# Deformable convolutions on one core: in the last layer, sampling two sources of an image in one column tile of 64, and one sum over taps for both

## The reference

```python
def _block(x, dc_w, dc_b, of_w, of_b, dw, db):
    h = jax.nn.relu(_deconv2d(x, dc_w, dc_b))          # 3x3, 32 -> 32 channels
    offset = _conv2d(h, of_w, of_b, PAD)               # 3x3, 32 -> 18 channels
    return jax.nn.relu(_deform_conv2d(h, offset, dw, db))
...
in_module = x                                          # 8 images, 32 channels, 64 x 64
x = _block(x, ...)
in_prev = 0
for i in range(1, 4):
    in_cur = x + in_prev
    x = _block(in_cur, ...)
    in_prev = in_cur
x_cat = jnp.concatenate((x, in_module), axis=1)        # 64 channels
offset = _conv2d(x_cat, fin_off_w, fin_off_b, PAD)
return _deform_conv2d(x_cat, offset, fin_dcn_w, fin_dcn_b)
```

## Time and profile before

| | |
|---|---|
| median of 3 runs | 4814.95 us (4804.08 to 4822.14) |
| profiled execution | 4836.05 us, span 4834.3 us |
| PE busy | 4162.3 us (86%), 73184 records |
| PEld busy | 3178.2 us (66%) |
| DVE busy | 2924.5 us (60%) |
| ACT busy | 2780.4 us (58%) |
| POOL busy | 1143.2 us (24%) |
| mean granted clock of PE | 0.904 |
| DMA | 533.42 MB, mean 110 GB/s |

### The profile page before, as it was taken

One profiled execution on the slowest core, in us unless ns is written; L12 is line 12 of the kernel. 1 busy time (PEld: TensorE's weight loads), 2 busy tenths in 40 slices (PEclk: granted clock), 3 DMA queues, 4 the chain that ended last, 5 costly groups with the idle time before them and its releaser, 6 DMA issues.

```text
span 4834.3 us, 204328 instructions
## 1 busy us (share of the span) xinstructions
PE 4162.3 (86%) x73184; PEld 3178.2 (66%) x73184; DVE 2924.5 (60%) x5838; ACT 2780.4 (58%) x6651; POOL 1143.2 (24%) x655
## 2 busy tenths in 40 slices
PE   4997997898898799798799699688888887888887
PEld 3775675676576576476577477476666765677776
DVE  4784784785685686586487488354444435455554
ACT  2893884785686596487498388243333333344443
POOL 0440341341342242243143144011111101111110
PEclk8998998899899899799799799888888898889899
DMA  3442442442442442443344344644444436444443
GB/s 123 119 125 75 121 126 73 120 125 70 124 125 76 116 125 77 109 125 97 97 125 112 85 125 121 172 114 102 109 97 111 102 86 164 109 112 114 114 114 77
DMA packets 253669, 533.42 MB, mean 110 GB/s; under 512 B 61488, under 2 KB 161328, under 8 KB 235824
## 3 DMA queue, kind: packets, MB, share of 16 engines
q1 hardware_dynamic: 253072, 524.86, 42.1%
HBM read 468.16 MB, written 56.45 MB: 109 GB/s over the span
## 4 chain that ended last, share of the span: by engine, by line
PE 74%; issue 9%; SPq 8%; DMA 3%; ACT 2%; DVE 2%; POOL 1%; POOLq 1%; ACTq 0%; DVEq 0%
PE P L534 26%; PE PS L548 25%; PE PS L560 16%; PE P L505 6%; SPq L386 4%; SPq L378 3%; DMA HB<-off_store 1%; ACT H L805 1%; DMA off_store<-FOFF 1%; PE PS L505 1%; DVE FOFF L989 1%; ACT YC L742 1%; DVE ST L993 0%; DVE ST L992 0%; DMA VT<-ht_store 0%
## 5 line engine op out<-in xcount | busy, mean ns | idle before, releaser
L872 DVE TENSOR_TENSOR A<-P,YC 121x384 f32<-121x384 f32 (+1 forms) x4608 | 2313.0, 550 | 1311.8 <-ACT YC L742 932.5
L534 PE MATMUL P<-HL,SEL 32*121 32x384 f16 (+1 forms) x21504 | 1618.6, 313 | 366.9 <-issue 266.6
L742 ACT ACTIVATE YC<-P 121x384 f32<-121x384 f32 (+1 forms) x4608 | 1727.1, 439 | 115.4 <-PE P L534 103.5
L534 PEld LDWEIGHTS P<-HL,SEL 32*121 32x121 f16 (+1 forms) x21504 | 1061.6, 119 | 775.9 <-issue 454.2
L548 PE MATMUL PS<-A,VT 121*32 121x144 f32 (+1 forms) x32768 | 1353.6, 305 | 114.8 <-issue 82.8
L548 PEld LDWEIGHTS PS<-A,VT 121*32 121x32 f32 (+1 forms) x32768 | 971.5, 115 | 451.6 <-issue 207.1
L1053 POOL CAST HL<-DIST 128x1152 f16<-128x1152 f32 x320 | 365.7, 1143 | 3430.1 <-DVE DIST L877 3365.3
L719 ACT ACTIVATE SMP<-PS 128x432 f32<-128x432 f32 (+1 forms) x1152 | 567.0, 492 | 717.9 <-PE PS L548 716.7
L560 PE MATMUL PS<-SMP,CW 128*128 128x128 f32 x6912 | 862.0, 281 | 5.2 <-ACT SMP L719 5.2
L560 PEld LDWEIGHTS PS<-SMP,CW 128*128 128x128 f32 x6912 | 800.9, 193 | 88.4 <-issue 77.5
L1055 POOL TENSOR_TENSOR HL<-DIST,HL 128x1152 f16<-128x1152 f32 x320 | 769.1, 2403 | 133.8 <-issue 74.5
(11 more groups left out here) (56 smaller groups left out, 580.8 us busy)
## 6 DMA issues: line engine op xcount, KB each, us to landing
HB<-off_store SPq DMA_DIRECT2D x2560, 72.0 KB, 2.5
VT<-ht_store SPq DMA_DIRECT2D x256, 512.0 KB
VT<-ht_store SPq DMA_DIRECT2D x768, 132.0 KB
VT<-ht_store SPq DMA_DIRECT2D x256, 88.0 KB
ht_store<-A SPq DMA_DIRECT2D x80, 256.0 KB, 3.5
off_store<-FOFF SPq DMA_DIRECT2D x160, 128.0 KB, 2.5
A<-x_dram SPq DMA_DIRECT2D x2, 2048.0 KB, 10.1
H<-x_dram SPq DMA_DIRECT2D x2, 2048.0 KB, 15.5
```

The costliest lines, as they stand in the source:

```text
L534: mm = nc.tensor.matmul(dst, SEL[q, table, 0:sh.npos], hats, start=part == 0, stop=part == 1)
L742: nc.scalar.activation(YC[0:sh.npos, g % X_SLOTS, 0:sh.size], P[0:sh.npos, g % Y_SLOTS, 0:sh.size], ACT.Copy).then_inc(y_ready, 1)
L872: return nc.vector.tensor_tensor(dst, x, y, ALU.mult)
```

## The change

In the last layer both sources of an image now share a column tile of 64 columns: `sample` multiplies the window's 64 channels (source 0's 32 and source 1's 32) at once, and the result takes 64 partitions of `PS`. Two images lie beside each other on the 128 partitions; the other pair of images goes to the next 144 columns. A unit is now a block and a pair of images instead of a block and a source. There are as many units, each of two products per tile of positions instead of four.

In `deform` a sampled column now holds both sources of two images, so one product per tap takes both sources. Its weights are 128 by 64: two blocks of 64 by 32, one per image. A chunk has 9 taps times 2 pairs, again 18 products; pair 0 writes partitions 0 to 63 of the bank, pair 1 writes 64 to 127, and each half adds up nine.

For this the channels of a pixel in DRAM are ordered image, source, channel instead of source, image, channel. ACT writes the transposes into the staging buffer at places of 32 channels, source 1 beside source 0, and the buffer is `A` for the first half of the rows and `VT` for the second. The stores to DRAM can only start when source 1's copies are there: ten stores in unit 1 with rows of 256 values, instead of ten in unit 0 and ten in unit 1 with rows of 128. The summing weights are one load of 128 by 576 values instead of two of 128 by 1152. The layers compute as before.

```diff
-        CW = sb("CW", [128, 2, TAPS * 128])
+        CW = sb("CW", [128, TAPS * 128])
...
-        def staged(source):
-
-            return (A if source == 0 else VT)[:, :, :].rearrange("p a b -> p (a b)")
+        def staged(sources, unit, n, count):
+
+            width = 512 * sources
+            return (A if unit == 0 else VT)[:, :, :].rearrange("p a b -> p (a b)")[0:count, width * n:width * (n + 1)]
...
-        def vt_tile(sh, buf, tile, w, source):
-            n = (tile * BLOCKS + w) * sh.sources + source
-            return VT[0:sh.npos, buf, 128 * n:128 * (n + 1)]
+        def vt_tile(sh, buf, tile, w):
+
+            width = sh.sources * 128
+            at = (tile * BLOCKS + w) * width
+            return VT[0:sh.npos, buf, at:at + width].rearrange("p (i c) -> p i c", i=IMG)
...
-                    for s in range(2):
-                        sp.dma_start(CW[:, s, :], t["fin_dcn_w"][s]).then_inc(sum_loaded, 16)
+                    sp.dma_start(CW[:, 0:TAPS * 64], t["fin_dcn_w"]).then_inc(sum_loaded, 16)
...
+            def store_ht(sources, unit, n):
+
+                sp.wait_ge(ht_copied, (UNITS * (sources - 1) + unit) * BANKFULS + n + 1)
+                first, count = sheet(unit, n)
+                width = sources * 128
+                dst = bass.AP(ht_store[sources - 1].ap().tensor, (MARGIN * LANE_COLS + first) * width,
+                              [[width, count], [LANE * width, LANES], [1, width]])
+                sp.dma_start(dst, staged(sources, unit, n, count).rearrange("p (t c) -> p t c", c=width)).then_inc(ht_stored, 16)
...
-                    for n in range(BANKFULS):
-                        if final:
-                            store_ht(sources, unit, 0, n)
-                        else:
-                            store_ht(sources, 0, unit, n)
-                    if final:
+
+                    for half in range(UNITS) if final and unit == 1 else [] if final else [unit]:
                         for n in range(BANKFULS):
-                            store_ht(sources, unit, 1, n)
+                            store_ht(sources, half, n)
...
-                wait_alone(sp, ht_stored, 16 * BANKFULS * UNITS * sources)
+                wait_alone(sp, ht_stored, 16 * BANKFULS * UNITS)
...
-                        for img in range(IMG):
-                            q = slice(CH * img, CH * (img + 1))
+                        vt = vt_tile(sh, vt_buf, n, 0 if same_window else first + w)
+                        for i in range(IMG // sh.sources):
+                            img = pair * (IMG // sh.sources) + i
+                            wide = CH * sh.sources
                             mm = nc.tensor.matmul(
-                                PS[q, 144 * v:144 * v + 144].rearrange("p (k y x) -> p k y x", k=TAPS, y=BLK),
-                                vt_tile(sh, vt_buf, n, 0 if same_window else first + w, source)[:, q],
+                                PS[wide * i:wide * (i + 1), 144 * v:144 * v + 144].rearrange("p (k y x) -> p k y x", k=TAPS, y=BLK),
+                                vt[:, img, :],
                                 a[:, TAPS * img:TAPS * (img + 1), :, at:at + BLK],
                                 start=n == 0, stop=n == sh.tiles - 1)
...
             def deform(sh, smp):
-                products = [(s, k) for s in range(sh.sources) for k in range(TAPS)]
-                for n, (s, k) in enumerate(products):
-                    rhs = SMP[:, smp, 0:sh.smp_size].rearrange("p (w s k a) -> p w s k a", s=sh.sources, k=TAPS,
-                                                               a=BPX)[:, :, s, k, :]
-                    mm = nc.tensor.matmul(PS[:, 0:CPX], CW[:, s, 128 * k:128 * (k + 1)], rhs,
-                                          start=n == 0, stop=n == len(products) - 1)
+
+                wide = 128 // sh.sources
+                for k in range(TAPS):
+                    for pair in range(sh.sources):
+                        rhs = SMP[:, smp, 0:sh.smp_size].rearrange("p (w s k a) -> p w s k a", s=sh.sources, k=TAPS,
+                                                                   a=BPX)[:, :, pair, k, :]
+                        mm = nc.tensor.matmul(PS[wide * pair:wide * (pair + 1), 0:CPX], CW[:, wide * k:wide * (k + 1)], rhs,
+                                              start=k == 0, stop=k == TAPS - 1)
                 return mm
...
-                        nc.scalar.activation(staged(s)[0:count, place:place + 512],
-                                             bank((4 if final else 0) + use % 4)[0:count, :], ACT.Copy).then_inc(ht_copied, 1)
+                        dst = staged(sources, unit, n, count).rearrange("p (l i s c) -> p s (l i) c", l=LANES, i=IMG, s=sources)
+                        nc.scalar.activation(dst[:, s], bank((4 if final else 0) + use % 4)[0:count, :].rearrange(
+                            "p (l c) -> p l c", c=CH), ACT.Copy).then_inc(ht_copied, 1)
```

More of the change, by code:

```diff
@@ L515, in transposes @@
                         pe.wait_ge(ht_copied, use - 3)
-                    first, count, _ = sheet(unit, n)
+                    first, count = sheet(unit, n)
                     at = HP + LANES * first
@@ L537, in sample @@
             def sample(sh, a_buf, vt_buf, first, units, same_window=False):
-                for v, (w, source) in enumerate(units):
+                for v, (w, pair) in enumerate(units):
                     for n in range(sh.tiles):
```

23 lines of the change are left out of this document (9 added, 14 removed).

## The result

The changed kernel takes **4525.89 us** (median of 4 runs, 4516.99 to 4532.77). The kernel before takes 4818.55 (4 runs, 4804.08 to 4835.76). The ratio is 0.939, with a 95% interval of 0.9352 to 0.9429: faster. The forecast was 4500, in a range of 4420 to 4660.

The account below looks back on a forecast made before the run. PE was taken to bound the kernel, idle about an eighth of the last layer in instruction-fetch holes that also lower its clock. Loops 316 + other chunks 16 - staging 15 = 317; 4836 - 317 = 4519, times 0.9956: 4500 us, range 4420 to 4660.

Parts of the forecast that it names:

- (3) The code: PE's last-layer loop body, 1744 to 1232 records, no longer fetched anew: every hole gone, 316 us, shorter sum included.
- B: Rival: only the last-layer loop's branch misses, the mid-part hole goes, the chunk-start one stays; 4620 us, chance 0.12.
- C: Rival: all fetch holes in the last layer's loop stay; 4723 us, in the runs 4702, chance 0.11.
- (1) The sum: Last layer's sum over taps on two column tiles: 4.29 to 2.2 us, 2.0 a chunk, 64 x 2.0 = 128 us.
- rival D: Two 64-wide column tiles don't run together, sampling costs 8.0 us more a chunk; 5097, in the runs 5075, chance 0.05.
- (2) Sampling: Last layer's 16384 32-wide sampling records become 8192 64-wide ones; PE's time stays: 0.
- (4) Staging: Last layer's later, wider transpose stores delay the first sample 8 to 9 us a group; 15 us taken as cost.
- The loops and the unrolled chunks: Last layer: 28 loop chunks a group go from 26.4 and 24.9 to 20.0 us, 316; other 8 gain 2.0 each, 16.
- (5) DMA: Last layer's loop: DMA share rises from 0.56 to about 0.62 at 18.9 us a chunk, not a bound.
- Above 0.95: Sign to check: PE's clock in the last layer's loops above 0.95; at 0.86 the time is some 4600 us.
- the bounds 18.9 and 21.8: Limits in us for a hole-free last-layer loop chunk, at full clock and at clock 0.86; 20.0 taken.
- Rival A: Full clock as well in the last layer's loops: 56 chunks at 18.9 instead of 20.0 us; 4440 us, chance 0.15.

Follow-up runs that it names:

- Experiment 2: The changed kernel with sampling alone put back to 32-wide products, 1744 records a pass of PE's loop: 4815.05 us, ratio 0.997.
- Experiment 1: The changed kernel with four chunks instead of two per pass of PE's last-layer loop, 2464 records, same work: 4595.55 us, ratio 0.9524.
- experiment 5: The changed kernel with 32-wide sampling in every second chunk only, 1488 records a pass: 4555.19 us, ratio 0.9439.
- experiment 3: The changed kernel with the sum alone put back to 18 products of 128x128 weights: 4621.43 us, ratio 0.956.
- experiment 8: The changed kernel with ACT's next-chunk distances formed under the sum and the sum put back to 128x128 weights: 4508.86 us, ratio 0.935.
- 9: The changed kernel with distances under the sum, X and next input behind first windows, chunk 2's offsets earlier, DVE's residual after batch two's group 7: 4364.7 us.
- Experiment 4: The changed kernel with ACT's next-chunk distances, and DVE's clamp, moved from the chunk's start to under the sum: 4424.92 us, ratio 0.9168.
- experiment 10: The changed kernel with 32-wide sampling, 1744 records a pass, and ACT's next-chunk distances formed under the sum: 4822.67 us, ratio 1.0008.

## Why the prediction was right, step by step

**The whole.** The profiled execution went from a span of 4834.3 to 4517.3, 317.0 less; the sum had 317. That is luck. The layers took 10.1 us less (the last layer's first transpose comes at 3030.5 us instead of 3040.6), though nothing in them changed. In the seven other profiles here whose layers load and compute in the same order it comes between 3027 and 3039, so this is the spread of executions, and no gain. The last layer's groups, from first transpose on, went from 920.7 to 744.6 and from 873.0 to 742.2, together 306.9. In them the loops gained 17 us less than was said, and staging and the unrolled chunks made up 7 of that (both below). By the medians it is 293.

**(3) The code: right, and it is the bulk.** Every fetch hole went, 120 packets a group became 3, and the loop chunk is 19.84 and 20.05 us where 20.0 was said. Experiment 2 has everything of the change but the shorter code, and keeps 0.3% of the 6.1%. Experiment 1 has everything but it, and loses 70 us. In experiment 5 32-wide products cost nothing where nothing is fetched. Rivals B (the branch misses) and C (all holes stay) fall with the packets. The Trainium skill's rule of the 2-page window (Runtime: NRT & Kernel Launch, section "Instruction fetch mechanics") is contradicted by a body of 1232 records whose branch fetches nothing. But the step to "every hole gone" was a choice between two bounds. The reason given for it, that the old body fetches more than its own size, has no row behind it, since the sizes were themselves worked out from the fetched bytes. It came true with less margin than the forecast made it: the edge lies at about 1488 records, between 1232 and 1744.
**(1) The sum: duration right, worth too large.** 4.29 to 2.19 us, as said; rival D (no overlap) falls. But its worth is not 2.0 us times 64 wherever it stands: 95 us in the changed kernel (experiment 3), 84 with early distances (experiment 8), the full 2.1 us a chunk once the residual is out of POOL's way (9 against 8), and in the old loop only 22 us over both loops, where 56 x 2.1 = 118 were saved in work (experiment 2). The forecast put terms 1 and 3 into one chunk time, so this did not show in the total. The two terms do not simply add: the shorter sum pays in full only where the loop is no longer fetched anew.

**(2) Sampling: 0, right.** 24 records in 1.69 us, two tiles beside each other.

**(4) Staging: right in size, incomplete in kind.** The first sample came 6.1 and 4.6 us later, together 10.7, where 15 was taken and "8 to 9 us later" a group was said. But the step looked no further than the first sample. The offsets of chunk 2 stand behind the windows, and PE waits 4.62 and 5.38 us for them: 20.7 in all instead of 15.

**The loops and the unrolled chunks: each a little off.** From a group's first sum to its 29th, 28 chunks, it took 734.1 and 686.6 us and takes 559.5 and 561.8: 299 gained, where 316 was said. The 26.4 and 24.9 us a chunk were means over 27 chunks and left out the first intervals, which have no hole at a branch (22.3 us in group 0, 20.8 and 20.9 in group 1). The rest of the groups, without staging, gained 18 with the two holes for offsets in it, where 16 was said.

**(5) DMA: right.** Share 0.58 in the loops; 0.61 to 0.64 at 17.6 to 18.6 us a chunk, and still no bound.

**Clock: the check was drawn too high.** "Above 0.95" was asked for and it is 0.93 and 0.92. With one wait of 1.1 to 1.4 us a chunk the clock drops in 48 chunks of 56. The argument from the unrolled chunks ("have that wait and run at full clock") did not carry over to the loop. The 20.0 was a choice between the bounds 18.9 and 21.8, not worked out, and that it came within 0.1 of the measured 20.0 and 20.1 is luck; the bounds were right. Rival A (full clock, 4440) did not happen by itself. Experiment 4 brought the full clock by taking the wait away: 4424.92.

## What to carry to other kernels

Look first whether PE's loop body is fetched anew (instruction packets in the loop, "issue" holes at fixed places). If so, first get the body short enough to stay: until then shorter products (experiment 2) and a wait less (experiment 10) gave next to nothing, and it is the number of records in the body that decides. When the body stays, small waits come next, since a wait can cost a drop of the clock behind it that is worth more than itself; here moving 1.25 us of ACT's work under the sum was worth 2.2%. After every gain look at what moved under what: the early distances together with the short sum brought a DVE instruction under POOL's, and that cost 0.9 us a chunk until it was moved. And look where an edit reaches: the offsets' place in SP's queue gave more in the layers than in the last layer, for which it was made. In a queue, a load moved back is late for someone, too: X, moved behind the windows, cost what the earlier windows gave.

## What the runs showed of the hardware

- A DVE instruction of three operands in SBUF (128x128) took 0.34 us alone, 2.53 us when it started with POOL's 2.38 us TENSOR_TENSOR at 3388.96, and 0.44 us when it started 0.3 us before that one's end. The mean of 24 in 3240 to 3700 us of experiment 4 was 2530 ns. By the Trainium skill (SBUF — State Buffer, section "SBUF: two separate sides") a DVE instruction with two SBUF inputs and a GpSimd one that reads SBUF exclude each other for a whole instruction; the trace agrees: in both cases the residual ended 0.14 us after POOL's instruction (3391.49 against 3391.35, and 3392.98 against 3392.84). In experiment 4 it was recorded as starting 0.01 us before POOL's and still ended after it, so the recorded starts do not tell which of the two has the right of way.
- A loop body of 1744 records that is fetched anew costs some 50 us a pass, whether its work is long or short (51.6 us in experiment 2, 49.1 and 51.5 in experiment 10), and one of 1488 records, where it is fetched anew, 51.7 to 53.5. One of 2464 records, with the same number of products a chunk as one of 1232, waits once a pass for 6 us. Why it has no hole in the middle stays open, as does what starts and ends the fetching at 1488.
- Two column tiles of 64 columns ran fully beside each other in fp32: 36 records in 2.19 us against 4.29 for 36 of 128 columns, with one product as long in both.
